# Quantised feed-forward: the layer norm joined to the stage, squares and statistics on ScalarE, the residual on TensorE

## What is computed

```python
def _layernorm(x, axis=-1, eps=1e-05):
    m = jnp.mean(x, axis=axis, keepdims=True)
    v = jnp.var(x, axis=axis, keepdims=True)
    return (x - m) / jnp.sqrt(v + eps)

def fp4_quant_dequant(x):          # along the last dim, BLOCK = 16
    xb = x.reshape(shape[:-1] + (shape[-1] // BLOCK, BLOCK))
    scale = jnp.max(jnp.abs(xb), axis=-1, keepdims=True) / 6.0
    scale = jnp.maximum(scale, jnp.float32(1e-12))
    xn = xb / scale
    idx = jnp.searchsorted(_MID, jnp.abs(xn))
    q = _GRID[idx] * jnp.sign(xn) * scale

gate = fp4_linear(x, w_gate)       # both operands quantised, 128 -> 352
y = fp4_linear(x, w_up)
h = jax.nn.silu(gate) * y
return fp4_linear(h, w_down)       # 352 -> 128

x = x + _L2_ffn_ref(_layernorm(x, axis=-1), ...)
```

## Time and profile before

| | us |
|---|---|
| median of 3 runs | 5079.56 (5078.65 to 5098.07) |
| the profiled execution | 5094.06 |
| its span in the trace | 5092.2 |
| l3fb: norm, from the first statistics to the first scale | 25.2 |
| l3fb: main part, to the last residual add | 177.2 |

### The profile page before, as it was taken

The page is one execution under the profiler, slowest core; times in us unless marked ns, Lnnn a source line. Parts: engine busy times, 40 slices in busy tenths (PEclk is TensorE's granted clock), DMA queues, the critical chain, the costliest instruction groups (busy, mean ns, idle before and its releaser), DMA issues. The chain is left out here.

```text
span 5092.2 us, 68375 instructions
## 1 busy us (share of the span) xinstructions
PE 3099.1 (61%) x23645; PEld 1890.2 (37%) x23645; DVE 2908.8 (57%) x6195; ACT 1598.7 (31%) x2718; POOL 2136.3 (42%) x2749
## 2 busy tenths in 40 slices
PE   5646346676266222855757774657756588746856
PEld 4546311111165112744643332423324233334534
DVE  4513447774423586235136665956749566478668
ACT  2212135564012110322213552225532144512621
POOL 6542411100332403222334445734459444377577
PEclk9768668887587555877767996769977599867877
DMA  5022132220121001100112210022200122000000
GB/s 139 36 63 59 27 88 66 57 59 1 45 66 52 21 0 42 56 19 4 57 31 77 69 52 1 1 62 69 74 2 0 48 60 71 27 1 1 1 1 17
DMA packets 218170, 206.27 MB, mean 41 GB/s; under 512 B 50439, under 2 KB 195015, under 8 KB 217080
## 3 DMA queue, kind: packets, MB, share of 16 engines
q1 hardware_dynamic: 205560, 176.85, 12.6%
q0 software_dynamic: 12288, 25.19, 1.7%
HBM read 103.55 MB, written 96.47 MB: 39 GB/s over the span
## 5 line engine op out<-in xcount | busy, mean ns | idle before, releaser
L829 DVE TENSOR_REDUCE l0b_negm<-l0b_ps_s 128x2 f32<-128x1024 f32 x256 | 302.8, 1220 | 167.9 <-PE l0b_ps_s L626 167.3
L708 ACT ACTIVATE l0b_E<-l0b_ps_t 128x1024 f32<-128x1024 f32 x256 | 262.0, 1023 | 222.6 <-PE l0b_ps_t L608 222.4
L829 DVE TENSOR_REDUCE l3a_negm<-l3a_ps_s 128x2 f32<-128x256 f32 (+3 forms) x256 | 199.1, 818 | 107.1 <-PE l3a_ps_s L632 106.7
L829 DVE TENSOR_REDUCE l2a_negm<-l2a_ps_s 128x2 f32<-128x256 f32 (+3 forms) x256 | 199.0, 818 | 100.4 <-PE l2a_ps_s L632 100.0
L829 DVE TENSOR_REDUCE l2b_negm<-l2b_ps_s 128x2 f32<-128x256 f32 (+3 forms) x256 | 199.0, 818 | 91.7 <-PE l2b_ps_s L632 91.2
L708 ACT ACTIVATE l3a_E<-l3a_ps_t 128x768 f32<-128x768 f32 (+1 forms) x192 | 169.2, 881 | 189.2 <-PE l3a_ps_t L608 188.8
L708 ACT ACTIVATE l2a_E<-l2a_ps_t 128x768 f32<-128x768 f32 (+1 forms) x192 | 169.4, 882 | 184.4 <-PE l2a_ps_t L608 184.1
L708 ACT ACTIVATE l2b_E<-l2b_ps_t 128x768 f32<-128x768 f32 (+1 forms) x192 | 169.4, 882 | 152.5 <-PE l2b_ps_t L608 152.3
L775 POOL TENSOR_SCALAR_AFFINE_SELECT l3a_E<-l3a_E 128x256 f32<-128x256 f32 x256 | 101.5, 409 | 232.2 <-ACT l3a_E L708 230.0
L775 POOL TENSOR_SCALAR_AFFINE_SELECT l2a_E<-l2a_E 128x256 f32<-128x256 f32 x256 | 101.5, 409 | 228.3 <-ACT l2a_E L708 225.9
L775 POOL TENSOR_SCALAR_AFFINE_SELECT l2b_E<-l2b_E 128x256 f32<-128x256 f32 x256 | 101.4, 410 | 222.5 <-ACT l2b_E L708 222.4
(11 more groups left out here) (997 smaller groups left out, 9554.6 us busy)
## 6 DMA issues: line engine op xcount, KB each, us to landing
l0b_stack<-l0b_q_piece SPq DMA_DIRECT2D x48, 128.0 KB
l0b_stack<-l0b_k_piece SPq DMA_DIRECT2D x48, 128.0 KB
room_up<-l0b_stack SPq DMA_DIRECT2D x32, 192.0 KB, 3.4
room_down<-l0b_stack SPq DMA_DIRECT2D x32, 192.0 KB, 4.4
l2a_stack<-l2a_q_piece SPq DMA_DIRECT2D x48, 128.0 KB
l2a_stack<-l2a_k_piece SPq DMA_DIRECT2D x48, 128.0 KB
room_up<-l2a_stack SPq DMA_DIRECT2D x32, 192.0 KB, 3.9
room_down<-l2a_stack SPq DMA_DIRECT2D x32, 192.0 KB, 4.8
```

The costliest lines, as they stand in the source:

```text
L708: act.activation(probs(n % 3, c, 0)[:, 2 * p:2 * p + 2, :], ps_t[:, :, 0:width[c]], ACT.Exp, scale=scale).then_inc(probs_ready.sem, 1)
L829: e = dve.tensor_reduce(negm[:, qt, :, j], ps_s[n % 2][:, :, off:off + keys[qt]], AX.X, ALU.max, negate=True)
```

## The change

`norm_stage` is no longer called ahead of the four feed-forward stages; its transposes and the XNT copies are not done there. Inside `quantized_ffn_stage`:

- DVE takes the statistics of batches 0 and 1 as before. For batches 2 to 7 ScalarE sums each row of X (`row_sums`: a Copy with scale -1/128 and a sum, then a Square with the mean as bias and a sum), DVE turns the sum of squares into a variance (`row_variance`), POOL takes the root (`roots`) and DVE the shift (`row_shift`). ScalarE writes XN (`normalise`, four operations a batch).
- POOL's product x_v is taken out of `quantize_x` into `scale_x(u)`, emitted behind `quantize_x(u-2)`; x_v and x_square have two buffers. The square is made by ScalarE (`squares`).
- TensorE adds X to ps_o by a product with the identity; ScalarE copies ps_o to X (`read_out`) where DVE added.

Apart from this, the attention stages take some DMA semaphores from a shared set with running counts in place of their own.

```diff
@@ load_stage and heads_attention_stage @@
+    core.pieces_stored = [Landed(core, f"{n}_pieces_stored") for n in "qk"]
...
-        pieces_stored = [own.enter_context(nc.semaphore(f"{name}_{n}_pieces_stored")) for n in "qk"]
...
+        pieces_stored, stack_ready, max_placed, ones_placed = core.pieces_stored, core.stack_ready, core.max_placed, core.ones_placed
...
@@ quantized_ffn_stage @@
+        stats = sb("stats", [P, 2 * TB, 6])
...
-        x_v = sb("x_v", [P, NX, BLOCK])
-        x_square = sb("x_square", [P, NX, BLOCK])
+        x_v = [sb(f"x_v{u}", [P, NX, BLOCK]) for u in range(2)]
+        x_square = [sb(f"x_square{u}", [P, NX, BLOCK]) for u in range(2)]
...
+        def tiles(b):
+            return slice(b * TB, (b + 1) * TB)
         @block.gpsimd
         def _(pool):
             ch = Chain(pool_step, pool, 0)
+            def roots(b):
+                pool.wait_ge(row_stats_ready.sem, row_stats_ready.upto(b + 1))
+                pool.tensor_tensor(rstd[:, tiles(b)], var[:, tiles(b)], core.minus_half[:, 0:TB],
+                                   ALU.pow).then_inc(row_rstd_ready.sem, 1)
+            def half(u):
+                return slice(u % 2 * NX, (u % 2 + 1) * NX)
+            def scale_x(u):
+                pool.wait_ge(x_inv_ready.sem, x_inv_ready.upto(u // 2 + 1))
+                if u >= 2:
+                    pool.wait_ge(xq_ready.sem, xq_ready.upto(u - 1))
+                pool.tensor_tensor(x_v[u % 2][:, :, :], blocks(x_tiles(u)), wide(x_inv[u // 2 % 2][:, half(u)], NX),
+                                   ALU.mult).then_inc(scaled_ready.sem, 1)
             def quantize_x(u):
+                v, square = x_v[u % 2][:, :, :], x_square[u % 2][:, :, :]
                 if u >= 1:
                     pool.wait_ge(xq_ready.sem, xq_ready.upto(u))
                 if u >= 2:
                     pool.wait_ge(xqT_in_psum.sem, xqT_in_psum.upto(u - 1))
-                pool.wait_ge(x_inv_ready.sem, x_inv_ready.upto(u // 2 + 1))
-                half = slice(u % 2 * NX, (u % 2 + 1) * NX)
-                ch.link(pool.tensor_tensor(x_v[:, :, :], blocks(x_tiles(u)), wide(x_inv[u // 2 % 2][:, half], NX), ALU.mult))
-                ch.link(pool.tensor_tensor(x_square[:, :, :], x_v[:, :, :], x_v[:, :, :], ALU.mult))
-                pool.tensor_scalar(x_power[:, :, :], x_square[:, :, :], 4.0, MAGIC, ALU.is_ge, ALU.mult)
-                ch.link(pool.tensor_scalar(x_square[:, :, :], x_square[:, :, :], 16.0, 2.0 * MAGIC, ALU.is_ge, ALU.mult))
-                ch.link(pool.tensor_tensor(x_power[:, :, :], x_power[:, :, :], x_square[:, :, :], ALU.add))
+                pool.wait_ge(squares_ready.sem, squares_ready.upto(u + 1))
+                pool.tensor_scalar(x_power[:, :, :], square, 4.0, MAGIC, ALU.is_ge, ALU.mult)
+                ch.link(pool.tensor_scalar(square, square, 16.0, 2.0 * MAGIC, ALU.is_ge, ALU.mult))
+                ch.link(pool.tensor_tensor(x_power[:, :, :], x_power[:, :, :], square, ALU.add))
                 ch.link(pool.tensor_scalar(x_power[:, :, :], x_power[:, :, :], MAGIC, None, ALU.add))
-                ch.link(pool.tensor_tensor(x_v[:, :, :], x_v[:, :, :], x_power[:, :, :], ALU.add))
-                ch.link(pool.tensor_tensor(x_v[:, :, :], x_v[:, :, :], x_power[:, :, :], ALU.subtract))
-                pool.tensor_tensor(blocks(xq[u % 2][:, :, :]), x_v[:, :, :], wide(x_scale[u // 2 % 2][:, half], NX),
+                ch.link(pool.tensor_tensor(v, v, x_power[:, :, :], ALU.add))
+                ch.link(pool.tensor_tensor(v, v, x_power[:, :, :], ALU.subtract))
+                pool.tensor_tensor(blocks(xq[u % 2][:, :, :]), v, wide(x_scale[u // 2 % 2][:, half(u)], NX),
                                    ALU.mult).then_inc(xq_ready.sem, 1)
+            roots(0)
+            roots(1)
+            scale_x(0)
+            scale_x(1)
             for u in range(ALL):
                 quantize_x(u)
+                if u % 2 == 1 and (u + 3) // 2 < B:
+                    roots((u + 3) // 2)
+                if u + 2 < ALL:
+                    scale_x(u + 2)
             pool_step.per = ch.k
         @block.vector
         def _(dve):
             ch = Chain(dve_step, dve, 0)
+            def row_statistics(b):
+                for n in range(b * TB, (b + 1) * TB):
+                    e = dve.bn_stats(stats[:, n, :], core.X[:, n, :])
+                ch.link(e)
+                for n in range(b * TB, (b + 1) * TB):
+                    e = dve.bn_aggr(mv[:, n, :], stats[:, n, :])
+                ch.link(e)
+                dve.tensor_scalar(minus_mean[:, tiles(b)], mv[:, tiles(b), 0], -1.0, None, ALU.mult)
+                dve.tensor_scalar(var[:, tiles(b)], mv[:, tiles(b), 1], LN_EPS, None, ALU.add).then_inc(row_stats_ready.sem, 1)
+            def row_variance(b):
+                dve.wait_ge(row_mean_ready.sem, row_mean_ready.upto(4 * (b - 1)))
+                dve.tensor_scalar(var[:, tiles(b)], deviation[:, tiles(b)], 1.0 / D, LN_EPS, ALU.mult,
+                                  ALU.add).then_inc(row_stats_ready.sem, 1)
+            def row_shift(b):
+                dve.wait_ge(row_rstd_ready.sem, row_rstd_ready.upto(b + 1))
+                dve.tensor_tensor(shift[:, tiles(b)], minus_mean[:, tiles(b)], rstd[:, tiles(b)],
+                                  ALU.mult).then_inc(row_bias_ready.sem, 1)
             def scales_x(b):
+                dve.wait_ge(row_norm_ready.sem, row_norm_ready.upto(b + 1))
                 sc, i = x_scale[b % 2][:, :], x_inv[b % 2][:, :]
                 if b >= 2:
                     dve.wait_ge(xq_ready.sem, xq_ready.upto(2 * (b - 1)))
...
                 quantize(ch, dve, blocks(hq[u % 2][:, :, :]), blocks(h[:, :, :]), v[:, :, :], power[:, :, :], scale[:, :],
                          inv[:, :]).then_inc(quant_ready.sem, 1)
-            def add(u):
-                x = core.X[:, u * T2:(u + 1) * T2, :]
-                dve.wait_ge(out_ready.sem, out_ready.upto(u + 1))
-                dve.tensor_tensor(x, x, ps_o[:, :, :], ALU.add).then_inc(out_read.sem, 1)
+            row_statistics(0)
+            row_statistics(1)
+            row_shift(0)
+            row_shift(1)
             scales_x(0)
             scales_x(1)
+            row_variance(2)
             for u in range(ALL):
+                if u % 2 == 0 and u // 2 + 2 < B:
+                    row_shift(u // 2 + 2)
+                if u % 2 == 1 and (u + 5) // 2 < B:
+                    row_variance((u + 5) // 2)
                 for t in range(T2):
                     multiply(u, t)
                 if u % 2 == 1 and u // 2 + 2 < B:
                     scales_x(u // 2 + 2)
                 quantize_h(u)
-                if u >= 1:
-                    add(u - 1)
-            add(ALL - 1)
             dve_step.per = ch.k
         @block.tensor
...
                 if u >= 1:
                     pe.wait_ge(out_read.sem, out_read.upto(u))
                 for t in range(T2):
+                    pe.matmul(ps_o[:, t, :], core.identf[:, :], core.X[:, u * T2 + t, :], start=True, stop=False)
                     for c, (lo, hi) in enumerate(CHUNKS):
                         mm = pe.matmul(ps_o[:, t, :], hT[u % 2][0:hi - lo, c, t * P:(t + 1) * P], w_outT[0:hi - lo, c, :],
-                                       start=(c == 0), stop=(c == 2))
+                                       start=False, stop=(c == 2))
                 mm.then_inc(out_ready.sem, 1)
             transpose_x(0)
...
                 lo, hi = CHUNKS[2]
                 act.activation(hT[u % 2][0:hi - lo, 2, :], ps_h[0:hi - lo, 1, 0:W], ACT.Copy).then_inc(quantT_ready.sem, 1)
+            def read_out(u):
+                act.wait_ge(out_ready.sem, out_ready.upto(u + 1))
+                act.activation(core.X[:, u * T2:(u + 1) * T2, :], ps_o[:, :, :], ACT.Copy).then_inc(out_read.sem, 1)
+            def row_sums(b, pair):
+                n0 = b * TB + 2 * pair
+                for n in (n0, n0 + 1):
+                    e = act.activation(seen[:, n % TB, :], core.X[:, n, :], ACT.Copy, scale=-1.0 / D, accum_out=minus_mean[:, n:n + 1])
+                e.then_inc(row_mean_ready.sem, 1)
+                act.wait_ge(row_mean_ready.sem, row_mean_ready.upto(4 * (b - 2) + 2 * pair + 1))
+                for n in (n0, n0 + 1):
+                    e = act.activation(seen[:, n % TB, :], core.X[:, n, :], ACT.Square, bias=minus_mean[:, n:n + 1],
+                                       accum_out=deviation[:, n:n + 1])
+                e.then_inc(row_mean_ready.sem, 1)
+            def normalise(b):
+                act.wait_ge(row_bias_ready.sem, row_bias_ready.upto(b + 1))
+                for n in range(b * TB, (b + 1) * TB):
+                    e = act.activation(core.XN[:, n, :], core.X[:, n, :], ACT.Identity, bias=shift[:, n:n + 1], scale=rstd[:, n:n + 1])
+                e.then_inc(row_norm_ready.sem, 1)
+            def squares(u):
+                act.wait_ge(scaled_ready.sem, scaled_ready.upto(u + 1))
```

(25 more changed lines are left out.)

72 lines of the change are left out of this document (48 added, 24 removed).

## The result

| | before | after |
|---|---|---|
| median | 5082.9 us (4 runs) | 5189.3 us (4 runs, 5184.5 to 5201.4) |
| the profiled execution, its span | 5094.1, 5092.2 | 5201.4, 5199.7 |
| one stage, l3fb, from the first statistics to the last write of X | 202.4 | 228.3 |
| first xq after the first statistics | 34.5 | 14.5 |
| the fifteen intervals of xq together | 146.1 | 191.1 |

The changed kernel is slower: ratio 1.0207, 95% interval 1.0179 to 1.0236, that is +106 us, where +93 was forecast. l3fb lengthens by 25.9 us and l2fb, from 201.6 to 227.9, by 26.3; the changed l2fa and l3fa take 227.5 each (before, a weights stage lay between their norm and their main part). Four times 26 us is 104 of the 107.5 us between the two spans.

What follows compares the result with a forecast made beforehand. DVE and POOL, both working without pause, bound the kernel. A stage: 14 + 7 + 9.7 + 83.5 + 14.5 + 74.6 + 22.4 = 225.7 us against 202.4; four stages +93, forecast 5173 us, range 5105 to 5230.

Steps and rivals of the forecast that it cites:

- The start: Stage start, two-batch statistics replacing norm_stage: first xq at 14 us, not 34.5; next intervals 7 and 9.7 us.
- Odd-to-even steps: From an odd round's xq to the next even one's: 2.85 waiting plus 7.8 quantisation, 10.65 us against 9.74, seven times.
- the quantisation beside DVE: POOL's seven operations from x_power to xq while DVE is busy: taken as 7.8 us, between 6.3 and 8.2.
- Even-to-odd steps: From an even round's xq to the next odd one's, waiting for the norm chain: 16.7 us, the last 14.5.
- the third loop: DVE's row_variance(b+1), ahead of its multiplies, waits for ScalarE's row_sums behind normalise(b), holding scales_x; within the 16.7 us step.
- the second one: Once a batch POOL's scale_x waits about 8 us for x_inv, as ScalarE's normalise(b) begins only after xq(2b-2).
- The end: From the sixteenth xq to the last residual write: 21.85 us plus 0.5 for the residual on TensorE.
- the fourth rival: TensorE's residual lengthens rounds on a slow clock, 10.5 against 10.65; if binding by 0.5, 14 us; chance 0.78 with the forecast.
- (1): Rival: ScalarE has norm data and squares ready before POOL asks; -24.4 us a stage, 4982 us; chance 0.08.
- (2): Rival: only POOL's wait for the squares holds, the norm chain being early enough; -10.8 us a stage, 5036; chance 0.04.
- the squares' loop: Every round POOL waits after xq for TensorE's transposes, then ScalarE's read_hT and square: 2.85 us before quantising.
- (3): Rival: the forecast's loops, but new offsets leave POOL and DVE hardly disturbed, quantisation 6.5 us; +41 in all, 5121; chance 0.08.

Runs made afterwards that it cites:

- the queue order in which it is nearly true: Changed kernel with squares early, row_variance and row_shift behind quantize_h, the norm's work two rounds sooner, a third scales buffer and scales_x one round sooner: 5013.5 us, 0.9852.

## Why the prediction was right, point by point

5189.3 us lies 16 above the forecast of 5173, in its range and on its side. By its steps, for l3fb (225.7 forecast, 228.3 measured):

- **The start**: 14.5 (14), then 7.1 (7) and 10.1 (9.7). Right. The first half microsecond is ScalarE's: normalise runs at 0.40 us an operation and not at 0.30.
- **Odd-to-even steps**: 2.98 + 8.1 = 11.1 (2.85 + 7.8 = 10.65) five times; the last two steps are 10.0 and 10.1. The path is right; the mis-sized term is **the quantisation beside DVE**, 8.1 in every steady round. I had put it between 6.3 and 8.2, as DVE "will be at work for most of it". In the trace DVE's quantize_h starts 0.9 us ahead of x_power in the even-to-odd step and 0.5 ahead in the other, since both wait for work that starts at the same xq, and POOL's last four operations meet DVE's long ones each time. 8.2, the only row with both at work, was the better choice. Only in the last two rounds does it take 7.0 and 7.4 (and 8.4 in the third).
- **Even-to-odd steps**: 16.6 in four (16.7), 17.5 in the first, 14.2 in the last (14.5). Misses cancel: TensorE and ScalarE were round in 2.2 us (to the end of the square) and not 2.75, normalise and row_sums took 3.1 and not 2.55; multiplies, scales, hand-overs and product came out 0.4 shorter, the quantisation 0.3 longer. That the total is right to 0.1 owes something to luck. The late row_variance confirms the third loop (2.4 us), the run with the norm ahead the second one (3.5 us more).
- **The end**: 22.8 (22.35). Over a stage all this is 2.6 us, 10 of the 16 us; another 3 are the median of before, now 5082.9 and not 5079.6.
- **TensorE's residual**: nothing in the rounds, as said. TensorE waits for xq in every one of the 16 rounds (86.0 us in all, the first of the waits above), so it binds none of them, and the residual alone on the kernel before is no slower either: the fourth rival falls. No run takes the residual out of the changed kernel.
- **The clock** is lower, as said, but by little: 0.75 from the first xq on (the row below), where the same stretch before had 0.78.

```profile
4976.50:5190.50 214.00, 125.79 (x512) 93.80 (x512) 149.25 (x227) 66.42 (x207) 125.73 (x125) 0.75 0.00 1
```

The **rivals**. (1), ScalarE ready in time, was priced at 4982. It is not what this change does, but the queue order in which it is nearly true reaches 5013.5. The price had counted 4.4 us a stage of faster rounds, and those never came: DVE and POOL stay at 20.5 us a pair. The prediction's own opening had it that whoever saves on both engines gains; no run bears that out. (2), the squares' loop alone at 5036, measured 5056.7 in its nearest form, the norm ahead: steps of 10.7 and 11.1, the quantisation again 8.1 to 8.6 and a last wait for x_inv left. (3), another offset, falls for the changed kernel: 8.1 in all but three of its rounds with both engines at work. It would have been wrong to rule it out, though: in the run with the square alone, the quantisation was 7.0 to 8.1. The exclusive lock of the Trainium skill, "SBUF — State Buffer", section "SBUF: two separate sides", is in line with a price that depends on how starts fall; the measured prices are 6.3 us with DVE idle, about 7.4 in one phase, and 8.1 to 8.4 in the other. POOL's two comparisons (1.08, 1.07 alone) are longer than that in 3 of 32 cases in the changed kernel's l3fb, and in 16 of 32 with the square alone. The prediction says that its rows show both sides losing; they show POOL's side, and DVE's is in the runs only.

One statement of the prediction was too strong. It gives the squares' loop a price of its own, 10.65 against 9.74. **On the kernel before no price can be told** (1.0011 with the wait and 0.9999 without, the intervals overlapping), and so it is with the other loops open: where POOL has a later wait in the same pair of rounds, or where the wait moves POOL's operations out of DVE's way, a wait of 1 to 2 us costs nothing. It was worth 0.9 us a pair in the changed kernel, where the even-to-odd step with its 8 us of waiting took up only 0.1 of it.

How much an offset is worth for the seven operations can be read across the twelve kernels that quantise h. In l3fb, by the start of quantize_h against the start of x_power:

| quantize_h starts | rounds, kernels | the seven operations |
|---|---|---|
| 0.8 us behind | 18, 6 | 8.4 us |
| 0.5 to 0.6 behind | 19, 4 | 8.2 |
| 0.1 to 0.4 behind | 6, 3 | 8.5 to 8.9 |
| 0 to 0.2 ahead | 19, 6 | 8.4 |
| 0.3 to 0.4 ahead | 17, 6 | 8.2 |
| 0.85 to 0.88 ahead | 41, 8 | 8.1 |
| 1.3 to 3.1 ahead | 25, 9 | 7.0 to 7.8 |

The same offset gives the same length in kernels with different queue orders, so here the offset goes with the price, and no offset seen brings it near 6.3 (the shortest with both at work is 6.8, once). What stays open is what a shift would be worth in the time of a stage. In the run with the square alone DVE also waits for the gates (0.38 and 0.66 us ahead of the multiplies that follow the round shown), and POOL's wait grows by about what its operations lose; no run shifts the one without the other.

## What to carry to other kernels

When work moves to an idle engine, follow that engine's queue, not its busy share: an operation placed behind one that waits for the result of the waiting engine closes a loop, and here the order alone was worth 3.0%, 5189 against 5034 us, with the same instructions, and 3.5% with a third buffer for the scales. Where two engines are both full and disturb each other, don't count an operation taken off one of them as time won: here it won nothing off POOL, nothing off DVE, and nothing in the fastest kernel either, where both were relieved. Price the operations beside the neighbour at the row where both work, unless the trace says when they don't.

## What the runs showed of the hardware

- Seven chained POOL operations of 128x256 in fp32 take 6.3 us with DVE nearly idle, 8.1 to 8.4 (8.9 at most) where DVE's chain of 128x704 operations starts within 0.9 us of them on either side, and 7.0 to 7.8 where it starts 1.3 to 3.1 us earlier. Both sides are longer: in the changed kernel POOL's last ones take 1.18, 1.25 and 1.15 (0.72, 0.72 and 0.62 alone), and DVE's two-input ones 1.30 at the same time (0.89 alone, as in the last round of the changed kernel, below).
- A relieved DVE stays as busy: 39.4 of 41 us with or without its residual adds, 0.41 us each, four in that stretch. The longer operations above count as busy in full, so the busy time of these two engines overstates their work.
- ScalarE's operations on 128 fp32 columns start 0.40 us apart with a scale and a bias taken from memory (normalise, 1.64 for four). A sum along the row costs a second record of 0.19 behind each: Copy with a sum starts every 0.29 us, Square with bias and sum every 0.40.

```profile
5183.24 0.89 DVE L2568 TENSOR_TENSOR l3fb_hq<-l3fb_v,l3fb_scale 128x704 f32<-128x704 f32 x1
```
